# A graph layer's second edge loop: TensorE's sums moved from the first to the last place of its step

## What is computed

```python
h = gelu(edge_scalar_attr @ W_mlp1 / sqrt(RADIAL))      # first layer
h = gelu(h @ W_mlp2 / sqrt(HID))                        # second layer
w00, w01, w10, w11 = h @ Wp_00, h @ Wp_01, h @ Wp_10, h @ Wp_11   # weights
out0_a = w00 * e0 * ea0
out0_b = w11 * sum(e1 * ea1[:, None, :], -1) * INV_SQRT3
out1_a = (w01 * e0)[:, :, None] * ea1[:, None, :]
out1_b = w10[:, :, None] * e1 * ea0[:, :, None]
n0, n1 = segment_sum(mid0, edge_dst), segment_sum(mid1, edge_dst)   # sums
```

## Time and profile before

| | us |
|---|---|
| median of 3 runs | 5571.94 (5563.18 to 5574.56) |
| the profiled execution | 5537.74 |
| its span, first to last instruction | 5536.0 |
| TensorE matmul busy | 3748.7 (68%) |
| DVE busy | 3229.4 (58%) |
| ACT busy | 1795.8 (32%) |
| GpSimd busy | 3393.7 (61%) |
| mean granted TensorE clock | 0.818 |

### The profile page before, as it was taken

One profiled execution on the slowest core, in us unless ns is written; L12 is line 12 of the kernel. 1 busy time (PEld: TensorE's weight loads), 2 busy tenths in 40 slices (PEclk: granted clock), 3 DMA queues, 4 the chain that ended last, 5 costly groups with the idle time before them and its releaser, 6 DMA issues. The chain is left out here.

```text
span 5536.0 us, 64081 instructions
## 1 busy us (share of the span) xinstructions
PE 3748.7 (68%) x14998; PEld 2529.6 (46%) x14998; DVE 3229.4 (58%) x10179; ACT 1795.8 (32%) x5061; POOL 3393.7 (61%) x3252
## 2 busy tenths in 40 slices
PE   2566666667676766776747777677677676775865
PEld 2244444444444444444435555455454554554644
DVE  3344555555555555555546666566676675664856
ACT  1244444444444444444432222122222221221221
POOL 4455555555555555555447776667676767766764
PEclk6787888888888888888867888778787887887877
DMA  5343443434443434444311111111111111111111
GB/s 173 108 114 101 112 113 108 112 108 106 112 110 105 113 108 114 112 112 112 84 50 43 42 43 42 45 44 44 42 43 44 43 40 46 43 41 44 44 43 54
DMA packets 322951, 431.52 MB, mean 78 GB/s; under 512 B 127443, under 2 KB 212647, under 8 KB 322440
## 3 DMA queue, kind: packets, MB, share of 16 engines
q0 software_dynamic: 103168, 211.49, 14.7%
q1 hardware_dynamic: 219256, 215.77, 13.9%
q10 hardware_dynamic: 144, 0.05, 0.0%
HBM read 410.36 MB, written 16.65 MB: 77 GB/s over the span
## 5 line engine op out<-in xcount | busy, mean ns | idle before, releaser
L219 POOL DMA_INDIRECT ahead_rows<-feat,c_src_tiles x1612 | 1827.1, 1133 | 815.6 <-issue 493.4
L181 POOL DMA_INDIRECT ring_rows<-xl,c_src_tiles x1612 | 1534.9, 952 | 1178.5 <-DVE attn_msg L1092 647.8
L932 PE MATMUL attn_sums_ps<-attn_msg,attn_onehot 128*128 128x136 f32 x3224 | 551.0, 324 | 726.9 <-DVE c_acc_attn L1033 526.1
L1585 PE MATMUL conv_sums_ps<-conv_vals,conv_onehot 128*128 128x256 f32 x3224 | 914.3, 433 | 108.2 <-issue 57.3
L1623 ACT ACTIVATE conv_scaled<-conv_w_ps,c_xT 128x64 f32<-128x64 f32 x1612 | 373.5, 314 | 1758.0 <-remote 807.0
L1592 PE MATMUL conv_w_ps<-c_Wp,conv_hid 128*128 128x256 f32 x1612 | 491.1, 433 | 618.9 <-ACT conv_hid L1629 345.1
L932 PEld LDWEIGHTS attn_sums_ps<-attn_msg,attn_onehot 128*128 128x128 f32 x3224 | 483.6, 223 | 781.6 <-issue 769.6
L1585 PEld LDWEIGHTS conv_sums_ps<-conv_vals,conv_onehot 128*128 128x128 f32 x3224 | 650.2, 212 | 338.7 <-issue 165.2
L981 ACT ACTIVATE attn_fifth<-attn_pre_ps,c_b_r 128x512 f32<-128x512 f32 x403 | 275.4, 683 | 1349.8 <-remote 779.8
L1098 DVE SCALAR_TENSOR_TENSOR attn_leaky<-attn_pre_ps,c_b_r,attn_fifth 128x512 f32<-128x512 f32 x403 | 301.3, 748 | 704.1 <-ACT attn_fifth L981 455.4
L1648 DVE TENSOR_SCALAR conv_onehot<-c_iota,c_dst_pos 128x128 f32<-128x128 f32 x1612 | 355.3, 297 | 608.0 <-remote 525.6
(11 more groups left out here) (221 smaller groups left out, 4685.4 us busy)
## 6 DMA issues: line engine op xcount, KB each, us to landing
c_xT<-in_attrT SPq DMA_DIRECT2D x403, 256.0 KB
attn_rel<-rel_group SPq DMA_DIRECT2D x403, 126.0 KB
ring_rows<-xl,c_src_tiles POOLq DMA_INDIRECT x1612
ahead_rows<-feat,c_src_tiles POOLq DMA_INDIRECT x1612
attn_xr_win<-xr_parts SPq DMA_DIRECT2D x403, 31.5 KB
ahead_radial<-in_radial_halves SPq DMA_DIRECT2D x101, 64.0 KB
attn_limit<-limit SPq DMA_DIRECT2D x403, 16.0 KB
xr_parts<-set_parts SPq DMA_DIRECT2D x13, 384.0 KB
```

Of the source, the lines that this page charges most:

```text
L181: pool.indirect_dma_start(self.rows[:, b, t, :], None, self.q["xl"][:, :], bass.IndirectOffsetOnAxis(ap=self.idx[:, bass.ds(k.index(TG, t) ...
L219: pool.indirect_dma_start(self.rows[:, k.slot(U), t, :], None, self.q["feat"][:, :], bass.IndirectOffsetOnAxis(ap=self.idx[:, bass.ds(k.in ...
L932: last = nc.tensor.matmul(to, onehot[:, g.slot(2), t, :], msg[:, g.slot(2), t, :, :].rearrange("p h o -> p (h o)"), start=wins > 1 or t == ...
L1585: last = nc.tensor.matmul(to, onehot[:, g.slot(2), t, :], vals[:, g.slot(2), t, :], start=wins > 1 or t == 0, stop=wins > 1 or t == TG - 1)
```

## The change

In the branch of TensorE's program shown above, the block under `if live(4)` (the sums) is moved from the head of the step to behind the block under `if live(0)`, ahead of the finishing pieces. No line of it is altered, and no other engine's program.

```diff
                 def body(k, live):
-                    if live(4):
-                        g = k.back(4)
-                        pe.wait_ge(vals_ready, g.uses())
-                        pe.wait_ge(onehot_ready, g.uses())
-                        at_least(pe, acc_steps, g.back(2 if wins == 1 else 1).uses(1, 2 * wins))
-                        for t in range(TG):
-                            to = sums_ps[:, g.slot(2), 0:DX] if wins == 1 else sums_ps[:, t // 2, t % 2 * DX:(t % 2 + 1) * DX]
-                            last = nc.tensor.matmul(to, onehot[:, g.slot(2), t, :], vals[:, g.slot(2), t, :], start=wins > 1 or t == 0, stop=wins > 1 or t == TG - 1)
-                        last.then_inc(sums_ready, 1)
                     if live(2):
...
                     if live(1):
...
                     if live(0):
...
+                    if live(4):
+                        g = k.back(4)
+                        pe.wait_ge(vals_ready, g.uses())
+                        pe.wait_ge(onehot_ready, g.uses())
+                        at_least(pe, acc_steps, g.back(2 if wins == 1 else 1).uses(1, 2 * wins))
+                        for t in range(TG):
+                            to = sums_ps[:, g.slot(2), 0:DX] if wins == 1 else sums_ps[:, t // 2, t % 2 * DX:(t % 2 + 1) * DX]
+                            last = nc.tensor.matmul(to, onehot[:, g.slot(2), t, :], vals[:, g.slot(2), t, :], start=wins > 1 or t == 0, stop=wins > 1 or t == TG - 1)
+                        last.then_inc(sums_ready, 1)
                     if wins == 1:
                         for j, piece, _ in fin_pieces(k.index()):
```

## The result

The changed kernel takes 5477.94 us (median of 4 runs, 5462.45 to 5488.89) against 5567.56 for the kernel before beside it: a ratio of 0.986, 95% interval 0.9824 to 0.9896. It is **1.4% faster**, where 2% slower was forecast. The profiled execution took 5481.15 us, its span is 5479.3.

The account below looks back on a forecast made before the run. No engine is full; the second loop alternates paced steps, where DVE locks out GpSimd's gathers, with holds. At 6.84 us a group, 403 x 0.28 = +113 us on 5537.7, plus 34 to the median, gave 5685; range 5330 to 5870.

Parts of the forecast that it names:

- The regimes: Second loop: paced steps with GpSimd's gather lead melting, lead gone, a costly stretch of late TensorE signals, then ragged recovery.
- point 3: DVE's longer step lets GpSimd start three gathers in 4.19 us, so the lead melts slower and lock time falls.
- Rival B: Port held as the skill's rule says: third gather delays L1679, step of 4.94 us, +192 us, 5764; chance 0.06.
- Point 2: DVE's one-hots wait for sums now last in TensorE's step: 4.19 us a step, 0.21 more; 42 us if all else stayed.
- The count of holds: Holds, stretches where TensorE's signals arrive late while gathers run without pause, come after n paced groups, n between 4 and 5.
- n = 4.5: Paced groups at 4.19 us between holds, taken between 4 and 5: 6.84 us a group; the turn is at n = 6.
- Rival A: Signals stay prompt at 1.40 us a gather, paced stretches longer: 5362 at n = 12 or 5222 at n = 28; chance 0.35.
- The price of a round: Paced groups, a hold's refill at 1.25 us a gather, 3.9 to release, 4.3 restart: (5.44 n + 13.2) / (n + 1) us a group.
- point 4: After a hold, at low clock, two groups each cost 1.6 us more and the release 1.1 more: 4.3 us a hold.
- Point 5: 39 finishing pieces now between sums and weights: at most 78 us, taken as 0 because the weights are 1.6 us early.
- The signs: Changed profile: 4.19 us steps, three gathers each, over 50 pauses, over 807 us remote, lock well under 305, no 3.98 stretches.

## Why the prediction was wrong

- **The regimes and point 3**: right. The third gather came (2.82 in steps under 4.8 us, by 2.21), lock time fell by 45%, and the runs of short steps went from 4.9 to 2.3 on average. Rival B wanted steps of 4.94 us; they are 3.98 and 4.40. The Trainium skill ("SBUF — State Buffer", section "SBUF: two separate sides") has a GpSimd instruction that reads SBUF, as a gather does for its indices, hold a two-input DVE instruction for its whole length if it comes first; L1679, 0.41 us behind a gather's start and on time, disagrees.
- **Point 2**: right in the mean. I had 4.19 us for each step; they mostly alternate, 87 under 3.99 (never two in a row) and 99 of 4.3 to 4.8 us. The mean of the 212 steps under 4.8 us is 4.23. The sums third, at a computed 3.88, stayed at 3.98.
- **The count of holds**: right in size. n = 4.5 means a hold in every 5.5 groups, 73 in the loop, and GpSimd paused 73 times. That the two are equal is luck: 65 of the pauses lie in or just behind a step over 8 us, and there are 86 such steps. Rival A needed longer paced stretches (n from 6 up) and is not what happened, though its sign is.
- **The price of a round**: this step failed. For 5.5 groups it was 37.7 us; measured are 35.2, and 73 x 2.5 = 182 us is about the 173 between +113 and -60.

| per pause | priced | measured |
|---|---|---|
| short steps | 2.5 x 4.19 = 10.5 | 2.9 x 4.23 = 12.3 |
| the restart's steps | 2 x 5.8 = 11.6 | 1.42 x 6.20 = 8.8 |
| the hold's step | 15.6 | 1.18 x 12.0 = 14.1 |

  The mis-sized term is **point 4, the restart**. In the sum, GpSimd gathers at 4.19 us for three or at 1.25 each, and on top of that a round has 3.9 + 4.3 = 8.2 us in which it starts nothing. Measured, it pauses 364.1 / 73 = 4.99 us. The 3.2 us too many are those that point 4 charges for two steps of 5.8 us. GpSimd doesn't stand still in such steps: in the 104 steps of 4.8 to 8 us it starts 4.45 gathers each, not three, and what it starts there the next hold needn't refill. The steps are shorter too: behind the 71 holds of the changed kernel (a step over 8 us with one under 8 behind it) the next two take 4.42 and 5.78 us on average, 1.8 above two of 4.19. Without the 3.2 the sum is (5.44 x 4.5 + 10.0) / 5.5 = 6.27 us a group, where 6.40 was measured. Most of what is missing, 0.6 us a round, is lock time and gaps: 45 us over the loop more than three gathers in 4.19 us leave room for. Break-even moves from n = 6 to 3.1, below my n. And little of the slow steps is the new order's: in the kernel with one more one-hot and the old order the two are 4.46 and 5.51 us, and in the kernel before they were 4.35 and 5.44, which its trace would have told. The timeline of the hold shows why the first is short: TensorE does its whole low-clock step, weights at 4380.50 to sums ending at 4389.40, inside the hold, so the first group behind the release doesn't wait for it. I had taken the step from one restart after a 51 us hold for all of them.

  The rest of the 8.2 us came out by luck. The sum counted 3.9 us to the release and 1.1 behind it, and left out the other 2.99 us from the release to L1686's end, which the hold's group needs as well. Measured over 68 of the 73 pauses, DVE's release comes 0.3 us behind the last gather's end on average (median 1.4), L1686 ends 4.0 later, as point 4 has it (4.05), and the next gather starts 0.8 after that. One miss is too long by 3.6, the other too short by about as much.
- The weighing failed with it: 4.3 of 37.7 us decided the sign, and that term was read from a single place. A hold with no such cost should have stood as a rival beside A.
- **Point 5** (finishing pieces at nothing): not tried by itself. The loop's 19.3 us on the chip without holds are the new lock time, which leaves nothing for it there.
- **The signs**: ACT's remote waits were to rise above 807 us and fell to 710. The other signs came as forecast: more than 50 pauses, three gathers in a step, less lock time, no stretches of 3.98 us steps.
- The forecast's time was 3.8% high; the measured one lies inside the range, which had been drawn down to take in A's nearer value.

The answer is not the same on every chip: the change gains 1.4% where there are holds and loses 0.8% where there are none.

**What beats both** where holds occur: before with three more one-hots a step, 0.962 to 0.965 of it. It is work for nothing and was not tried where there are no holds; what it shows is that there GpSimd's time in the step was worth more than DVE's speed.

## What to carry to other kernels

When an engine whose own work, gaps and pauses fill the loop is held up by a faster one through a shared port, lengthening the faster one's step can gain. Add up the slow engine's time first, lock and pauses apart, because a change can save one and pay with the other. Then look at how many of the slow engine's pieces fit between two locks, and whether one piece more is 0.02 us away. Where a regime of rounds is priced, the sign can hang on one term; take it from several restarts of the trace, and charge only time in which the slow engine does nothing. And time a change on more than one chip before keeping it.

## What the runs showed of the hardware that was not expected

- The same kernel took 5549 to 5653 us on some chips and 4304 to 4305 us on others, each time steady; the one chip that was met twice was of the same kind both times (5653 and 5549 us). Gather medians are the same (0.944 and 0.945 us), and gathers are 1.24 us apart in both. What differs is that TensorE's signals are late while gathers run close: 807 us of remote before ACT's scaling in the first trace, none in the others, and a granted clock of 0.82 against 0.94. The first loop, which gathers too, shrinks as well (2876 to 2192 us up to the second loop), and 780 us of remote before ACT's L981 are gone from it. The packets of the gathers' queue take as long on both, 126 and 129 ns on average. So gathers 1.24 us apart don't make a hold by themselves. What else it takes is open; nothing in the profile names it.
- Where holds occur, 0.09 us more between gathers took the steps over 8 us from 56 to 36, and with DVE's longer step from 40 to 17.
- A GpSimd memset of 128 x 128 values (0.22 us) behind a gather adds only 0.09 us to the distance of the gathers, and one of 128 x 256 (0.325) adds 0.20.
